# Another order of the beginning: quads 4 and 5 convolved ahead of W1's split, b2 split last, zero fills later

## The chip, the cores and the metric

One core of one Trainium2 chip runs the whole kernel. The metric is device time in microseconds, from the first to the last instruction and what little lies around them. Several executions are timed and their median is compared.

## What is computed

The kernel normalizes x (8192 rows of 128, in 128 graphs of 64 rows), runs one graph convolution with a residual, adds x again, normalizes once more, and runs a mixture of eight experts with two chosen for each row:

```python
n  = layernorm(x)
h  = layer_norm(n, ln_gamma, ln_beta)
x  = x + (n + relu(adj @ h @ W_rel + b_rel + h @ W_root))
m  = layernorm(x)
s  = m @ Wg.T + bg                  # 8 scores for a row
p, e = softmax over the 2 highest scores, and which experts they are
x  = x + sum over the two e of p * (relu(m @ W1[e].T + b1[e]) @ W2[e].T + b2[e])
```

x is 4.2 MB, adj 2.1 MB, W1 and W2 2.1 MB each, all fp32. The expert products are done with each operand split into a high and a low fp16 half.

## The kernel before

**Units.** A tile is 128 rows (two graphs), a quad is 4 tiles, and the 64 tiles lie in five groups of 8, 16, 16, 16 and 8 tiles (`GS`, line 24), so group 0 is quads 0 and 1, and group 1 is quads 2 to 5. A pass of the expert part (`p`) is 256 gathered rows of one expert.

**One quad's path.** DVE takes x's statistics (`stats_in`) and scales (`scales_in_first`, `scales_in_last`, 16 short dependent steps). DVE (`norm_in`) or ACT (`h0_make`) normalizes, ACT forms the first sum (`plus_norm`). PE transposes (`h0_transpose`), ACT copies out of PSUM (`hT_copy`), PE multiplies by W_rel (`relation`), ACT copies (`u_copy`), PE adds W_root and the adjacency product (`convolve`). DVE adds the result to X (`residual`), takes statistics (`stats_out`), makes scales for two quads at once in the beginning (`scales_out_first`, `scales_out_last`), and DVE or ACT normalizes again (`norm_out`). ACT writes the high halves (`split_high`), DVE the low halves (`split_low`), PE transposes (`xn_transpose`), ACT copies (`xnT_copy`), PE makes the scores (`score`), DVE copies them (`scores`). `pair_of_quads(n)` is residual to norm_out for quads n and n + 1.

**Routing of a group.** `route_first` and `route_second` find each row's two experts, PE counts them (`rank`), `route_slots` and `route_rows` turn that into row numbers (IDX, semaphore slots_made), `route_blocks` into the expert of each pass (experts_made) and the two weights. With IDX made, POOL writes the group's rows to HBM with 2 indirect DMAs for each tile (`scatter`, line 314). SP then loads them transposed (`load_rows`), PE runs the passes (`hidden`, `output`), ACT and DVE split the hidden layer (`high_half`, `low_half`), ACT copies and stores the result (`y_copy`, `store_y`), POOL fetches it for each row (`gather`, line 321), and DVE adds it (`combine`). The scattered rows of a group need their buffer in HBM filled with zeros first (`zero_rows`, 2.5 MB each, line 250).

**Weights.** W1 is split in 8 column blocks c of 512: PE multiplies by a masked identity (`weight_whole`), ACT writes the high half (`weight_high`), PE subtracts it (`weight_rest`), ACT writes the low half (`weight_low`); the 8 blocks go through PSUM banks `WB`, four at a time (`four_whole`, `four_rest`, `four_high`, `four_low`). W2 is split without PE: ACT `second_high`, DVE `second_low`, one per expert. b2 is split on one partition: two ACT copies and one DVE instruction at lines 841, 842 and 638.

**Order.** Every engine has its own written-out instruction list and waits on semaphores; nothing is planned by a program. The lists of the beginning are lines 255 to 283 for SP, 598 to 657 for DVE, 807 to 861 for ACT and 1022 to 1069 for PE. The loop over passes follows on each. Ahead of it PE waits for b1's rows, for both parts of b2 (`b2_made`, 2) and for the six quads' scores (`score_made`, 6); in pass 1, after `rank(1)`, it waits for all of W2's low halves (`w2lo_made`, 8). DVE has `route_slots(1)` and `route_rows(1)` at the end of its pass 0, after two low halves and 8 `stats_in` of group 2. The order of PSUM banks for quads 0 to 5 is given by `banks` (line 153): quad 2 has (PY, PH3), quad 3 (PH2, PC), quad 4 (PA, PB), quad 5 (PH0, PH1).

## Time and profile before

| | |
|---|---|
| median of 3 runs | 740.11 us (738.97 to 742.23) |
| the profiled execution | 739.89 us |
| its span, first to last instruction | 738.0 us |
| PE busy / weight loads | 397.4 / 332.7 us |
| DVE, ACT, POOL busy | 310.2, 241.7, 250.0 us |
| mean granted TensorE clock | 0.751 |
| first pass of the experts on PE | 86.33 us |
| indirect DMAs, POOL | 128 writing (44.43 us on), 128 reading |

A timeline row gives the start in us from the start of the span, the busy time of the merged instructions, engine, line, operation, output and inputs, shapes and count, and in brackets the idle time before it and what ended it. "issue" and "remote" (in the chain: "another core or an unknown queue") mean that nothing the profile shows ended the wait; on one core, "remote" is not another core. A wait's row in the list of waits gives total us, number of times, longest.

### The profile page before, as it was taken

The page shows a single profiled execution, that of the slowest core. Times are in us where ns is not written, and L with a number is a line of the kernel's source. Part 1 is how long each engine was busy: PE and PEld are TensorE (multiplying, and loading weights), DVE is VectorE, ACT ScalarE, POOL GpSimd, SP SyncE. Part 2 cuts the span into 40 slices and gives each one's busy share as a digit, 9 for nine tenths or more (in the row PEclk, how much of TensorE's full clock was granted, in tenths as well). Part 3 has the DMA queues.
Part 4 walks back from the last instruction along what each step waited for, and adds up shares of the span by engine and source line. Part 5 has one row for each costly group of instructions (what it writes and reads, how often), then busy time and mean ns, then how long its engine had stood idle before and what let it go on. Part 6 is the DMA issues. An engine that isn't in the chain of part 4 may idle for free.

```text
span 738.0 us, 12242 instructions
## 1 busy us (share of the span) xinstructions
PE 397.4 (54%) x3927; PEld 332.7 (45%) x3927; DVE 310.2 (42%) x1113; ACT 241.7 (33%) x519; POOL 250.0 (34%) x263
## 2 busy tenths in 40 slices
PE   4873652199728505987211139964801999415910
PEld 4652540198618404875100039853701887314700
DVE  6773870067707403568400005761400753203651
ACT  3875310178425202852100027621300553102300
POOL 2043047400340672002777700044375000672053
PEclk9996585599868855999655559995955899756965
DMA  9934022132221211133111123232331442421231
GB/s 306 368 142 116 0 54 82 33 73 66 55 64 38 78 50 50 36 79 73 50 53 53 50 61 73 64 75 61 73 82 43 112 117 62 104 53 47 67 106 53
DMA packets 86540, 59.48 MB, mean 81 GB/s; under 512 B 57426, under 2 KB 78546, under 8 KB 85844
## 3 DMA queue, kind: packets, MB, share of 16 engines
q1 hardware_dynamic: 56756, 31.23, 14.7%
q0 software_dynamic: 8192, 16.79, 8.0%
q10 hardware_dynamic: 21536, 10.69, 6.1%
q8 instruction: 38, 0.62, 0.3%
q14 instruction: 18, 0.15, 0.1%
HBM read 19.61 MB, written 28.38 MB: 65 GB/s over the span
## 4 chain that ended last, share of the span: by engine, by line
PE 40%; another core or an unknown queue 23%; issue 19%; DVE 9%; ACT 5%; POOL 2%; DMA 1%; ACTq 0%; SPq 0%; DVEq 0%; POOLq 0%
PE PH L990 6%; PE PY L1014 5%; PE PY L1019 5%; PE PY L1015 5%; PE PH L992 5%; PE PH L991 4%; PE PY L1006 2%; POOL YG L330 2%; PE PB L911 1%; ACT N L734 1%; DVE STI L384 1%; PE PA L919 1%; DVE HL L571 1%; PE PA L920 1%
## 5 line engine op out<-in xcount | busy, mean ns | idle before, releaser
L571 DVE SCALAR_TENSOR_TENSOR HL<-PH,HH 128x512 f16<-128x512 f32 (+1 forms) x168 | 108.4, 674 | 293.0 <-ACT HH L791 244.5
L317 POOL DMA_INDIRECT rows<-XHL,IDX x128 | 123.9, 968 | 264.5 <-DVE IDX L543 227.0
L330 POOL DMA_INDIRECT YG<-yrows,IDX x128 | 121.8, 951 | 211.8 <-DMA yrows<-YB 173.9
L791 ACT ACTIVATE HH<-PH 128x512 f16<-128x512 f32 (+1 forms) x168 | 95.6, 582 | 145.3 <-remote 95.8
L1015 PE MATMUL PY<-W2H,HL 128*128 x652 | 122.6, 231 | 18.5 <-issue 18.4
L1014 PE MATMUL PY<-W2H,HH 128*128 x652 | 122.6, 231 | 10.9 <-issue 10.7
L990 PE MATMUL PH<-XT,W1H 128*128 128x256 f16 (+1 forms) x396 | 107.1, 273 | 26.6 <-issue 24.8
L799 ACT ACTIVATE YB<-PY 128x256 f32<-128x256 f32 x84 | 31.8, 378 | 272.7 <-remote 167.2
L992 PE MATMUL PH<-XT,W1L 128*128 128x256 f16 (+1 forms) x396 | 106.1, 271 | 20.5 <-issue 20.5
L1019 PE MATMUL PY<-W2L,HH 128*128 x652 | 106.6, 231 | 18.0 <-issue 18.0
L991 PE MATMUL PH<-XT,W1H 128*128 128x256 f16 (+1 forms) x396 | 106.3, 271 | 17.4 <-issue 17.4
L1006 PE MATMUL PY<-B,KH 128*128 x99 | 27.0, 272 | 110.5 <-issue 62.7
L1015 PEld LDWEIGHTS PY<-W2H,HL 128*128 128x128 f16 x652 | 67.8, 104 | 15.8 <-issue 15.0
L1014 PEld LDWEIGHTS PY<-W2H,HH 128*128 128x128 f16 x652 | 67.4, 103 | 15.7 <-issue 13.2
L1019 PEld LDWEIGHTS PY<-W2L,HH 128*128 128x128 f16 x652 | 57.1, 104 | 23.2 <-issue 22.7
L1006 PEld LDWEIGHTS PY<-B,KH 128*128 128x128 f16 x99 | 10.0, 101 | 120.3 <-issue 118.8
L990 PEld LDWEIGHTS PH<-XT,W1H 128*128 x396 | 41.2, 104 | 46.8 <-issue 37.4
L992 PEld LDWEIGHTS PH<-XT,W1L 128*128 x396 | 40.8, 103 | 25.3 <-issue 20.5
L991 PEld LDWEIGHTS PH<-XT,W1H 128*128 x396 | 40.9, 103 | 23.1 <-issue 19.2
L590 DVE SCALAR_TENSOR_TENSOR X<-YG,PR,X 128x128 f32<-128x128 f32 x128 | 36.2, 347 | 17.2 <-DMA YG<-yrows,IDX 16.6
L460 DVE SCALAR_TENSOR_TENSOR XHL<-N,XHL 128x512 f16<-128x512 f32 x16 | 10.8, 690 | 47.3 <-issue 30.7
L727 ACT ACTIVATE X<-X,SHI,SC 128x128 f32<-128x128 f32 x64 | 26.1, 483 | 0.0
(186 smaller groups left out, 517.8 us busy)
## 6 DMA issues: line engine op xcount, KB each, us to landing
yrows<-YB ACTq DMA_DIRECT2D x37, 256.0 KB, 2.7
rows<-XT SPq DMA_DIRECT2D x2, 2496.0 KB, 15.5
YG<-in_w SPq DMA_DIRECT2D x2, 2048.0 KB, 11.8
out<-X SPq DMA_DIRECT2D x16, 256.0 KB
X<-in_x SPq DMA_DIRECT2D x3, 1024.0 KB, 5.5
ADJ<-in_adj SPq DMA_DIRECT2D x32, 64.0 KB, 3.2
rows<-XHL,IDX POOLq DMA_INDIRECT x128
YG<-yrows,IDX POOLq DMA_INDIRECT x128
```

What stands on the lines that cost most here:

```text
L317: nc.gpsimd.indirect_dma_start(rows[g % 2], bass.IndirectOffsetOnAxis(ap=IDX[:, col:col + 1], axis=0), XHL[:, src:src + 2 * P].bitcast(F32 ...
L330: nc.gpsimd.indirect_dma_start(YG[g % 2][:, dst:dst + P], None, yrows[g], bass.IndirectOffsetOnAxis(ap=IDX[:, col:col + 1], axis=0)).then_ ...
L571: nc.vector.scalar_tensor_tensor(layer(HL[:, at:at + 2 * BW], p), layer(PH[p % 2 * 2 + h][:, :], p), 0.0, layer(HH[:, at:at + 2 * BW], p), ...
L590: ins = nc.vector.scalar_tensor_tensor(tile(X, t), y, PR[:, pr:pr + 1], tile(X, t), ALU.mult, ALU.add)
L791: nc.scalar.activation(layer(HH[:, at:at + 2 * BW], p), layer(PH[p % 2 * 2 + h][:, :], p), ACT.Relu).then_inc((hia_made, hib_made)[h], 1)
L990: nc.tensor.matmul(o, wh, hi, start=True, stop=False)
L991: nc.tensor.matmul(o, wh, lo, start=False, stop=False)
L992: last = nc.tensor.matmul(o, wl, hi, start=False, stop=True)
L1006: nc.tensor.matmul(PY[:, k * n * P:(k + 1) * n * P], KH[:, H_B2M:H_B2M + P], b2, start=True, stop=False, skip_group_check=True)
L1014: nc.tensor.matmul(o, HH[:, at:at + P], wh, start=False, stop=False, skip_group_check=True)
L1015: nc.tensor.matmul(o, HL[:, at:at + P], wh, start=False, stop=False, skip_group_check=True)
L1019: last = nc.tensor.matmul(o, HH[:, at:at + P], wl, start=False, stop=c == C - 1, skip_group_check=True)
```

## The change

PE's list: after the scores of quads 0 and 1 come the transposes and relations of quads 4 and 5, `rank(0)`, and their convolutions; W1's split (both fours) follows, then quads 2 and 3's second transposes. W1's PSUM banks and waits change to fit. ACT's list: `h0_make(5)` ahead of `plus_norm(3)`; the copies of quads 4 and 5, `plus_norm(4)`, b1 and W1's first four; `plus_norm(5)` between its highs and lows; `norm_out(3)` and the split of quads 2 and 3 between the two fours; b2's copies after all quads, then `second_high` of experts 2 to 7 (0 and 1 earlier). DVE's list: `norm_in(4)` ahead of the scores of group 0; `residual` of quads 2 and 3 and their scales and `norm_out(2)` around `route_slots(0)` and `route_rows(0)`, ahead of `route_blocks(0)`; `residual` of quads 4 and 5 directly after b1; the low halves of W2 for experts 2 to 7 as one block at the end, behind group 1's first routing and b2. SP's list: the zero fill of buffer 0 after the adjacency loads of quads 4 and 5. `norm_in` has one wait more. Nothing is added to or taken from the computation.

```diff
--- before.py
+++ after.py
@@ -148,7 +148,7 @@
         PH = [pb(f"PH{k}") for k in range(4)]
         PY = pb("PY")
         PA, PB, PC = pb("PA"), pb("PB"), pb("PC")
-        WB = 2 * [PA, PB, PH[0], PH[1]]
+        WB = [PB, PH[1], PH[3], PC, PB, PH[1], PY, PH[2]]
 
         def banks(n):
 
@@ -267,10 +267,10 @@
             sp.dma_start(YG[1][:, :], w2[:, :]).then_inc(w2_in, 16)
             for r in (0, 32):
                 sp.dma_start(B2F[r:r + 1, :], b2[:, :]).then_inc(b2_in, 16)
-            zero_rows(0)
             for n in (4, 5):
                 sp.wait_ge(conv_done, n - 3)
                 load_adj(n)
+            zero_rows(0)
             zero_rows(1)
 
             sp.wait_ge(b1hi_made, 1)
@@ -410,6 +410,7 @@
                 if n >= 4:
                     dve.wait_ge(xnT_done, n - 3)
                     dve.wait_ge(xhi_made, n - 3)
+                    dve.wait_ge(xlo_made, n - 3)
                 for k in range(GT):
                     t = n * GT + k
                     at = 2 * T0[g] + GS[g] + t - T0[g]
@@ -623,38 +624,45 @@
             pair_of_quads(0)
             split_low(0)
             split_low(1)
+            norm_in(4)
             scores(0)
             scores(1)
             route_first(0)
             route_second(0)
-            norm_in(4)
+            residual(2)
+            stats_out(2, 0)
             route_slots(0)
             route_rows(0)
+            residual(3)
+            stats_out(3, 1)
+            scales_out_first(2, 2)
+            scales_out_last(2, 2)
+            norm_out(2)
             route_blocks(0)
 
             dve.wait_ge(b1hi_made, 1)
             nc.vector.scalar_tensor_tensor(B1L[:, :], B1F[:, :], W1S, B1H[:, :], ALU.mult, ALU.subtract).then_inc(b1lo_made, 1)
+            for i in range(2):
+                residual(4 + i)
+                stats_out(4 + i, i)
+            split_low(2)
+            split_low(3)
+            scales_out_first(4, 2)
+            scales_out_last(4, 2)
+            norm_out(4)
+            second_low(0, 2)
+            scores(2)
+            scores(3)
+            split_low(4)
+            split_low(5)
+            scores(4)
+            scores(5)
+            route_first(1)
+            route_second(1)
             dve.wait_ge(bt_made, 1)
             nc.vector.scalar_tensor_tensor(B2[32:33, :], B2F[32:33, :], YS / 64.0, BT[32:33, :],
                                            ALU.mult, ALU.subtract).then_inc(b2_made, 1)
-            pair_of_quads(2)
-            second_low(0, 1)
-            split_low(2)
-            split_low(3)
-            second_low(1, 2)
-            scores(2)
-            second_low(2, 3)
-            scores(3)
-            pair_of_quads(4)
-            second_low(3, 6)
-            split_low(4)
-            split_low(5)
-            second_low(6, 7)
-            scores(4)
-            second_low(7, 8)
-            scores(5)
-            route_first(1)
-            route_second(1)
+            second_low(2, 8)
 
             for p in range(NP):
                 for n, at in START.items():
@@ -828,36 +836,36 @@
                 split_high(n)
             for n in (0, 1):
                 xnT_copy(n)
+            h0_make(5)
             plus_norm(3)
-            h0_make(5)
-            four_high(0)
-            exp_gap(0)
-            four_low(0)
-            four_high(4)
-            four_low(4)
-            act.wait_ge(b1_in, 16)
-            nc.scalar.mul(B1H[:, :], B1F[:, :], W1S).then_inc(b1hi_made, 1)
-            act.wait_ge(b2_in, 32)
-            nc.scalar.activation(B2[0:1, :], B2F[0:1, :], ACT.Copy, scale=YS / 64.0).then_inc(b2_made, 1)
-            nc.scalar.activation(BT[32:33, :], B2F[32:33, :], ACT.Copy, scale=YS / 64.0).then_inc(bt_made, 1)
             for n in (4, 5):
                 hT_copy(n)
             for n in (4, 5):
                 u_copy(n)
-            second_high(0, 4)
+            exp_gap(0)
+            plus_norm(4)
+            act.wait_ge(b1_in, 16)
+            nc.scalar.mul(B1H[:, :], B1F[:, :], W1S).then_inc(b1hi_made, 1)
+            four_high(0)
+            plus_norm(5)
+            four_low(0)
             norm_out(3)
             for n in (2, 3):
                 split_high(n)
+            four_high(4)
+            four_low(4)
+            second_high(0, 2)
             for n in (2, 3):
                 xnT_copy(n)
-            for n in (4, 5):
-                plus_norm(n)
-            second_high(4, 8)
             norm_out(5)
             for n in (4, 5):
                 split_high(n)
             for n in (4, 5):
                 xnT_copy(n)
+            act.wait_ge(b2_in, 32)
+            nc.scalar.activation(B2[0:1, :], B2F[0:1, :], ACT.Copy, scale=YS / 64.0).then_inc(b2_made, 1)
+            nc.scalar.activation(BT[32:33, :], B2F[32:33, :], ACT.Copy, scale=YS / 64.0).then_inc(bt_made, 1)
+            second_high(2, 8)
             act.wait_ge(b2_made, 2)
 
             for p in range(NP):
@@ -943,8 +951,12 @@
 
             def weight_whole(c):
 
-                if c >= 4:
+                if c == 3:
+                    pe.wait_ge(rank_used, 1)
+                if c in (4, 5):
                     pe.wait_ge(wlo_made, c - 3)
+                if c >= 6:
+                    pe.wait_ge(conv_read, c - 3)
                 nc.tensor.matmul(WB[c][0:P - 1, :], KF[:, K_M:K_M + P - 1], YG[0][:, c * HID:(c + 1) * HID],
                                  start=True, stop=True).then_inc(w_done, 1)
 
@@ -1043,20 +1055,23 @@
                 xn_transpose(n)
             for n in (0, 1):
                 score(n)
+
+            pe.wait_ge(score_made, 2)
+            for n in (4, 5):
+                h0_transpose(n)
+            for n in (4, 5):
+                relation(n)
             pe.wait_ge(kh_in, 16)
+            rank(0)
+            for n in (4, 5):
+                convolve(n)
             pe.wait_ge(w1_in, 16)
-
-            pe.wait_ge(score_made, 2)
             four_whole(0)
-            rank(0)
             four_rest(0)
             four_whole(4)
             four_rest(4)
             pe.wait_ge(wlo_made, 8)
-            first_half(4, 5)
             for n in (2, 3):
-                if n == 3:
-                    pe.wait_ge(rank_used, 1)
                 xn_transpose(n)
             for n in (2, 3):
                 score(n)
```

## Rows read from the trace of the kernel before

**Rows 1.** The page, part 4: share of the span of the chain that ended last.

```profile
PE 40%; another core or an unknown queue 23%; issue 19%; DVE 9%; ACT 5%; POOL 2%; DMA 1%; ACTq 0%; SPq 0%; DVEq 0%; POOLq 0%
```

**Rows 2.** The list of waits from 98 us to the end, POOL's rows.

```profile
POOL rows L317 <- DVE IDX L543: 187.4, 4, 62.9
...
POOL YG L330 <- DMA yrows<-YB: 173.9, 4, 61.8
```

**Rows 3.** Busy times by stretch: W1's split, then two of POOL's runs of indirect DMAs.

```profile
core 0: us, PE busy (x) PEld busy (x) DVE busy (x) ACT busy (x) POOL busy (x), PEclk, DMA share, GB/s
33.40:45.70 12.30, 11.02 (x26) 4.62 (x26) 9.93 (x54) 9.47 (x21) 1.13 (x1) 0.87 0.14 57
44.40:66.20 21.80, 9.72 (x65) 7.79 (x65) 13.00 (x48) 11.17 (x21) 15.82 (x16) 0.87 0.47 170
98.90:144.00 45.10, 11.51 (x74) 7.03 (x74) 8.49 (x35) 1.62 (x4) 30.73 (x32) 0.58 0.21 60
```

**Rows 4.** Timeline of DVE, up to the first routing's end.

```profile
33.25 0.19 DVE L466 COPY LG<-PH 128x32 f32<-128x32 f32 x1 [0.70 <-PE PH L935]
...
38.81 0.22 DVE L504 COPY TOT<-PC 128x64 f32<-128x64 f32 x1 [1.17 <-PE PC L942]
...
43.96 0.17 DVE L543 CAST IDX<-SLF 128x16 int32<-128x16 f32 x1
...
46.54 0.19 DVE L636 SCALAR_TENSOR_TENSOR B1L<-B1F,B1H 128x32 f16<-128x32 f32 x1
```

**Rows 5.** Timeline of DVE, quads 2 to 5 and group 1's routing.

```profile
48.40 1.27 DVE L638 SCALAR_TENSOR_TENSOR B<-HL,HH 1x1024 f16<-1x1024 f32 x1 [1.66 <-issue]
...
52.83 0.17 DVE L373 TENSOR_TENSOR MEANO<-STO 128x8 f32<-128x8 f32 x1
...
56.52 1.11 DVE L453 TENSOR_SCALAR N<-X,SCO,SHO 128x127 f32<-128x127 f32 x4
...
60.77 1.29 DVE L460 SCALAR_TENSOR_TENSOR XHL<-N,XHL 128x512 f16<-128x512 f32 x2 [2.54 <-issue]
...
70.00 0.19 DVE L466 COPY LG<-PY 128x32 f32<-128x32 f32 x1 [7.34 <-PE PY L935]
...
79.43 1.88 DVE L580 SCALAR_TENSOR_TENSOR W2L<-YG,W2H 128x512 f16<-128x512 f32 x3
...
85.22 0.19 DVE L466 COPY LG<-PH 128x32 f32<-128x32 f32 x1 [0.92 <-PE PH L935]
...
92.31 0.28 DVE L504 COPY TOT<-PC 128x128 f32<-128x128 f32 x1
```

**Rows 6.** Timeline of ACT: b2's first copy, quad 2's second transpose, quads 4 and 5.

```profile
46.25 1.04 ACT L841 ACTIVATE B<-HL 1x1024 f16<-1x1024 f32 x1
...
67.45 0.59 ACT L758 COPY T<-PH 128x512 f32<-128x512 f32 x1 [6.19 <-remote]
...
78.40 1.64 ACT L734 ACTIVATE N<-X,SHO,SCO 128x127 f32<-128x127 f32 x4 [4.73 <-DVE SHO L446]
...
80.99 0.56 ACT L758 COPY T<-PB 128x512 f32<-128x512 f32 x1
```

**Rows 7.** Timeline of PE, start of the first pass.

```profile
86.33 0.39 PE L990 MATMUL PH<-XT,W1H 128*128 128x256 f16 x1 [1.14 <-DVE LG L466]
```

**Rows 8.** Timeline of POOL: first and 14th indirect DMA of group 0, first of group 1.

```profile
44.43 1.13 POOL L317 DMA_INDIRECT rows<-XHL,IDX  x1 [39.58 <-DVE IDX L543]
...
61.07 1.22 POOL L317 DMA_INDIRECT rows<-XHL,IDX  x1 [0.30 <-issue]
...
98.92 0.96 POOL L317 DMA_INDIRECT rows<-XHL,IDX  x1 [34.10 <-DVE IDX L543]
```

**Rows 9.** Timeline of SP's queue: first zero fill, first transposed loads.

```profile
13.95 0.62 SPq L252 DMA_DIRECT2D rows<-XT  x1
...
66.19 4.01 SPq L244 DMA_TRANSPOSE XT<-rows  x3
```

**Rows 10.** The page, part 2: traffic in slices of 18.45 us.

```profile
GB/s 306 368 142 116 0 54 82 33 73 66 55 64 38 78 50 50 36 79 73 50 53 53 50 61 73 64 75 61 73 82 43 112 117 62 104 53 47 67 106 53
```

## The prediction

> **What bounds the kernel now.** I read the chain that ended last first: 40% of it is PE's work, and 42% are "issue" and the unknown releaser, waits that nothing in the profile ends [rows 1]. Then the waits of POOL: its indirect writes wait for the row numbers IDX of each group, its reads for the stored results [rows 2]. Nothing behind the beginning waits for a fixed moment; each stage waits for the one before it. So what the beginning wins by the time POOL's second run of writes starts (98.92 us, [rows 8]) should come off the end one for one, unless stalls behind it change.
>
> The stalls have a pattern, in the busy times by stretch [rows 3]. While POOL works through a run of indirect DMAs, PE gets through about 70 matmuls (65 in 21.8 us, 74 in 45.1 us), then almost stops, and starts again when the run is over. In the first run one sees it begin: DVE pauses 2.54 us before a low half [rows 5], and ACT gets quad 2's transpose at 67.45 after 6.19 us [rows 6], 1.3 us after SP's first load, which itself waits for the scatter to land [rows 9]. In the old beginning PE has in this run both relations and both convolutions of quads 4 and 5 (48 matmuls), and 8 transposes before.
>
> Then I read DVE's timeline, since it carries the chain through the beginning: it waits 7.34 us for quad 2's scores up to 70.00 and ends the six quads' scores at 85.22; POOL's second run follows 13.70 us later [rows 5, 8].
>
> **The change, part by part.** I lay DVE's new list end to end, each piece with its old duration.
>
> To the first IDX: old, slots and rows run from 38.81 to 43.96 (5.15 us), behind 1.17 us of waiting for `rank(0)` and the 1.1 us of `norm_in(4)`, so routing's first half ended at 36.5 [rows 4, 5]. Now `norm_in(4)` falls into the waits for the first scores (0.70 us at 33.25 and a like one before it, [rows 4]). In its old place stand `residual(2)` and its statistics. Two quads' residuals and statistics run from the end of b2's instruction, 49.67, to 52.83 [rows 5], 1.58 each. So slots start at 36.5 + 1.58 = 38.1 and IDX is at 43.3, 0.7 earlier. On PE `rank(0)` now stands behind the transposes and relations of quads 4 and 5. From the scores at 33.4 ACT ends a sum (1.64) and a copy (0.6), and 16 matmuls follow at 9.72/65 = 0.15 [rows 3, 4, 6]: 38.0, just hidden. If it is 1 us late, so is all.
>
> From IDX on (43.4): `residual(3)` 1.58; scales of a pair 3.69 (52.83 to 56.52); `norm_out(2)` 1.1; `route_blocks(0)` with b1 2.7 (43.96 to 46.54 and 0.19) [rows 4, 5]; residuals of quads 4 and 5 3.16; two low halves 1.29; scales 3.69. That is 17.2 us, so the scales of quads 4 and 5 are there at 60.6; they were at 78.40 [rows 6]. From there to the last scores old needed 6.82 us (78.40 to 85.22) through ACT, PE and ACT [rows 5, 6]; DVE's own work beside it (norm 1.1, two W2 blocks at 0.63, two scores, two low halves 1.29) is 4.1 and fits. Last scores: 67.4, **17.8 us earlier**.
>
> Is ACT ready? Between 33.4 and 60.6 it has four normalizations or sums at 1.64, the 16 evictions of W1 at 9.47/16 = 0.59 or less, eight copies and splits and two W2 blocks at about 0.6: 22 us in 27 [rows 3, 6]. That leaves 5 us for its hand-overs with PE. b2's two ACT copies (1.04 each, [rows 6]) lie beside the last scores and the routing.
>
> What is paid back: group 1's row numbers used to follow the last scores by routing, low halves, statistics and slots, with no block of weights between (85.22, 92.31, 98.92). Now b2 (1.27) and six W2 low halves (six times 0.63 = 3.8) stand on DVE behind the routing and ahead of the first low half [rows 5]: **5.0 us given back**. PE itself starts when b2 is ready, at 67.4 + 4.2 + 1.3 = 72.9 against 86.33 [rows 7], 13.4 earlier, and its wait for W2 in pass 1 is over by then. The shift of POOL's second run is 17.8 - 5.0 = **12.8 us**.
>
> Zero fill: its issue moves from 13.95 [rows 9] to behind quads 4 and 5's adjacency, about 22 us. Old, all that was asked for in the first 24 us had moved by 37 us at 306 and 368 GB/s [rows 10]. Both fills (5.1 MB) from 22 us on take 14 us at the second rate and end at 36 to 38; POOL needs the first at 43.4. Hidden, with 5 us to spare; past that, each us late is a us of the end. The extra wait of `norm_in(4)` costs nothing, since the low half it names stands ahead of it on DVE.
>
> Not in this sum: stalls inside POOL's first run. Old they cost DVE 2.54 us and the chain 6.19. New, PE has fewer matmuls in it: by the code, of W1 the last block's two, four rests, eight wholes and four rests, then 24 for quads 2 and 3, 24 for quads 4 and 5: about 66, against the 65 that it got through before. So the limit is met only at the very end, if at all. Below the sum nothing is to be gained but PE at its higher clock there (the granted share is 0.87 in the first run's stretch, 0.58 in the second, [rows 3]). Above it: one pause like DVE's, 2.5 us. I take 0.8 us, nearer to none. Net: 12.0 us.
>
> A rule that speaks against it. POOL's DMAs of the first run come every (61.07 - 44.43)/13 = 1.28 us while DVE is busy 13.0 of 21.8 us, and one that meets DVE's low half takes 1.22 instead of about 0.96 [rows 3, 5, 8]. The Trainium skill (SBUF — State Buffer, "Who interferes with whom") says that a DVE instruction with two SBUF inputs and a GpSimd one that reads SBUF lock each other out for a whole instruction. DVE will be denser in this run, with four such low halves and two of W2; at the 0.26 us of the row each, the run would end 1.6 us later by the rule, and 0 by the even pace of the others. The run's end is off the chain of the sum, so neither changes it.
>
> **The rivals.**
> B, *PE's hand-overs of quads 4 and 5 are held to the end of the run.* Old, ACT got its transpose only 1.34 us behind the landing of the scatter [rows 6, 9]. With a run 0.7 us earlier that is 66.7, and from the first such copy to the last scores it is 80.99 to 85.22, 4.23 us [rows 5, 6]: last scores 70.9, 3.5 later than in the sum. Gain 12.8 - 3.5 = 9.3, span 728.7. For it: 66 matmuls are right at the limit, and completions lagged before PE stopped. Against: they are spread over 20 us here.
> C, *the gain is eaten behind the beginning.* The eight later sets of POOL's DMAs (four writing, four reading, each with its wait in [rows 2]) may meet PE at other points. If they turn out 6 to 9 us worse in sum, the span is 732 to 735. Against: from POOL's second run on the instruction lists are the same and their distances too.
> D, the slower side: *W1's split chokes inside the run.* Old, the split lay ahead of it (33.4 to 45.7, [rows 3]) and convolutions, which need one signal for four tiles, lay in it. Now twelve of sixteen evictions wait for PE's signal one by one, under the run. If these signals are held to its end from the first lows on (47 us in my layout), then 20.4 us of the way to the last scores start at 66.7: 87.1, 1.9 later than old, and with the 5.0 given back the span is 738 + 6.9 = 745. It decides from a first hold before about 50 us. Against: the W1 signals fall among the first 18 of the 65 matmuls that PE gets through before it is held [rows 3].
> E, *more*: PE stays at the higher clock to the last scores, and these come 2 to 3 us sooner (quads 4 and 5's eight transposes and sixteen score matmuls); 723.
> F, it doesn't do what it says: `rank(0)` behind the new work comes late enough to push IDX and everything back by the same; 1 to 2 us, inside the others' ranges.
>
> **How the numbers follow.** The likeliest is the sum: 738.0 - 12.0 = 726.0 us of span; the profiled execution has 1.9 us around its span, and the median stands 0.2 above the profiled 739.9. Forecast 728.1. Chances: sum (A) 0.45, B 0.27 (731), C 0.12 (734 to 737), D 0.08 (742 to 747), E 0.08 (725). From 722 to 736 holds A, B, E and half of C. About 0.5% (3.7 us) is what a measurement of this kernel can tell from no change: faster than 736.4 are A, B, E and most of C, 0.86; within, the rest of C and the mild part of D and stalls I don't see, 0.08; slower 0.06.
>
> **What would show it.** IDX's first copy at 43.3 and the first indirect DMA at about 43.7. Scales of quads 4 and 5 at 60.6 (ACT's L734, third time). Last L466 of the six at 67.4 (A) or about 71 (B). The first pass's matmul at 72.9, POOL's second run at 86.1. ACT's W1 rows without "remote" ahead of them; with 5 us or more of it there, D. The distance from POOL's second run to the end of the span is 639.1 us before; if it is within 2 us of that, C is out. If the second run starts at 86 and the span is still above 733, my step "one for one" is wrong; if it starts after 92, the layout of DVE's list or the stalls in the first run are.

## The result, and the profile after

The median went from 740.87 to 734.72 us (five runs each side, ratio 0.9917, interval 0.9898 to 0.9937). Another pair on another chip gave 744.96 and 739.77 us, ratio 0.9911 (0.9874 to 0.9948). So the change gains 5 to 6 us of time where 12 were forecast; the forecast median was 728.1. The profiled execution has a span of 733.4 us against 738.0.

| | before | after | forecast |
|---|---|---|---|
| first IDX copy | 43.96 | 45.30 | 43.3 |
| scales of quads 4 and 5 (SHO) | 78.20 | 68.87 | 60.6 |
| last scores of the six quads | 85.22 | 75.90 | 67.4 |
| first matmul of the first pass | 86.33 | 82.41 | 72.9 |
| POOL's second run starts | 98.92 | 94.66 | 86.1 |
| from there to the end of the span | 639.1 | 638.8 | 639.1 |

The timeline of DVE in the changed kernel, at the scales of quads 4 and 5 (start, duration, engine and line, operation; in brackets the idle time before it and what ended that):

```profile
58.02 0.68 DVE L461 SCALAR_TENSOR_TENSOR XHL<-N,XHL 128x512 f16<-128x512 f32 x1
58.62 0.21 DVE L373 TENSOR_TENSOR MEANO<-STO 128x8 f32<-128x8 f32 x1
...
59.23 0.17 DVE L377 SCALAR_TENSOR_TENSOR VARO<-MDIFO,VARO 128x8 f32<-128x8 f32 x1
59.97 0.17 DVE L437 TENSOR_SCALAR RAO<-VARO 128x8 f32<-128x8 f32 x1 [0.57 <-issue]
60.68 0.17 DVE L363 TENSOR_SCALAR RTO<-RAO 128x8 int32<-128x8 int32 x1 [0.54 <-DVE RAO L437]
61.40 0.17 DVE L364 TENSOR_SCALAR SCO<-RTO 128x8 int32<-128x8 int32 x1 [0.54 <-DVE RTO L363]
62.79 0.17 DVE L367 TENSOR_TENSOR RTO<-SCO 128x8 f32<-128x8 f32 x1 [1.22 <-DVE SCO L364]
...
68.60 0.17 DVE L369 SCALAR_TENSOR_TENSOR SCO<-RTO,SCO 128x8 f32<-128x8 f32 x1
68.87 0.17 DVE L447 SCALAR_TENSOR_TENSOR SHO<-MEANO,SCO 128x8 f32<-128x8 f32 x1
```

Up to 59.23 the steps start 0.2 us apart or closer; from 59.97 they are 0.70 or 1.40 apart, though each lasts 0.17 us, and at 68.60 they are 0.2 apart again. The chain of scales took 10.25 us (58.62 to 68.87) instead of 3.69. POOL's first run, in its timeline, frames this:

```profile
45.77 1.13 POOL L317 DMA_INDIRECT rows<-XHL,IDX  x1 [40.91 <-DVE IDX L544]
...
58.63 0.96 POOL L317 DMA_INDIRECT rows<-XHL,IDX  x1 [0.30 <-issue]
...
64.95 0.96 POOL L317 DMA_INDIRECT rows<-XHL,IDX  x1 [0.30 <-issue]
```

The steps slow down beside its twelfth DMA and recover 2.7 us after its last has been issued. Below, a "hold" is this: an engine starts its instructions late though nothing that the profile shows stands in their way. The windows of the changed kernel show the same by engine (stretch, its length, then busy time and number of instructions of PE, PE's loads, DVE, ACT and POOL, the granted clock of PE, DMA share, GB/s): up to 59 us the engines are dense, then DVE and ACT thin out, while PE has matmuls for 5.16 of the 7 us, at about half its clock. ACT's copy of quad 3's second transpose starts at 63.51, after 3.13 us of "issue"; PE's 8 matmuls that read it follow at 64.15. The last line is a stretch in POOL's second run, 21 matmuls in 32 us.

```profile
45.70:59.00 13.30, 9.20 (x24) 3.41 (x23) 12.20 (x54) 12.44 (x27) 10.19 (x11) 1.00 0.32 97
59.00:66.00 7.00, 5.16 (x24) 4.62 (x24) 1.52 (x9) 1.97 (x4) 5.39 (x6) 0.53 0.82 333
...
101.95:133.90 31.95, 5.44 (x21) 1.60 (x18) 1.72 (x5) 1.19 (x2) 24.04 (x26) 0.58 0.25 70
```

Behind the beginning, in the timelines of DVE, PE and POOL, which answer to [rows 7] and [rows 8]:

```profile
75.90 0.19 DVE L467 COPY LG<-PH 128x32 f32<-128x32 f32 x1 [1.52 <-PE PH L943]
...
80.44 1.22 DVE L663 SCALAR_TENSOR_TENSOR B<-HL,HH 1x1024 f16<-1x1024 f32 x1
...
82.41 0.39 PE L1002 MATMUL PH<-XT,W1H 128*128 128x256 f16 x1 [6.55 <-DVE B L663]
...
94.66 0.96 POOL L317 DMA_INDIRECT rows<-XHL,IDX  x1 [28.75 <-DVE IDX L544]
```

The last scores come 9.3 us earlier. From them to POOL's second run it is 18.76 us against 13.70: the 5.06 us of b2 and W2 that were given back.

### The profile page after: what moved, and what is told of

Its sections match the earlier page's. It is cut to its first block, busy times and chain, and to the rows that moved or that the text cites. A ratio compares the mean times of both kernels' runs of the same rounds, so it can differ in the third digit from the quotient of the medians.

```text
span 733.4 us, 12242 instructions
## 1 busy us (share of the span) xinstructions
PE 400.7 (55%) x3927; PEld 338.3 (46%) x3927; DVE 310.4 (42%) x1113; ACT 241.0 (33%) x519; POOL 249.8 (34%) x263
## 4 chain that ended last, share of the span: by engine, by line
PE 36%; another core or an unknown queue 20%; issue 20%; DVE 15%; ACT 5%; POOL 2%; DMA 2%; ACTq 0%; SPq 0%; DVEq 0%; POOLq 0%
PE PY L1026 5%; PE PH L1002 5%; PE PY L1031 5%; PE PY L1027 5%; PE PH L1004 4%; PE PH L1003 4%; PE PY L1018 2%; POOL YG L330 2%; PE PB L919 2%; DVE HL L572 2%; ACT N L742 1%; DVE STI L384 1%; ACT N L724 1%; DVE STO L431 1%
## 5 line engine op out<-in xcount | busy, mean ns | idle before, releaser
L1027 PE MATMUL PY<-W2H,HL 128*128 x652 | 124.1, 233 | 22.1 <-issue 21.9
L1026 PE MATMUL PY<-W2H,HH 128*128 x652 | 124.2, 233 | 16.0 <-issue 15.9
L1031 PE MATMUL PY<-W2L,HH 128*128 x652 | 108.1, 233 | 18.7 <-issue 18.7
L919 PE MATMUL PB<-WF,T 128*128 128x128 f32 x96 | 16.7, 330 | 21.1 <-ACT T L750 21.1
```

The lines of the kernel that those rows point to most:

```text
L1026: nc.tensor.matmul(o, HH[:, at:at + P], wh, start=False, stop=False, skip_group_check=True)
L1027: nc.tensor.matmul(o, HL[:, at:at + P], wh, start=False, stop=False, skip_group_check=True)
L1031: last = nc.tensor.matmul(o, HH[:, at:at + P], wl, start=False, stop=c == C - 1, skip_group_check=True)
```

## The experiments

Times of key instructions come from each kernel's profiled execution. "This chip's before" is the kernel before, run beside. Two theories stand at the start: R, POOL's run slows DVE's steps and that ate the gain (as S in the expectations, with one allowance of instructions for all engines together); X, the loads of later x, issued in this stretch, do it (DMA share 0.82 in the windows above). P stands for any cause on PE's side. Theory O, that the order was never worth what I wrote, came up on the way.

**e1_scatter_held**, the changed kernel, POOL's first run held until the six quads are scored:

```diff
                 pool.wait_ge(zero_out[g % 2], 16)
+                if g == 0:
+                    pool.wait_ge(score_made, 6)
```

> The changed kernel, but POOL's first run of indirect DMAs also waits for the scores of all six quads. Nothing is left out. In the changed kernel the 16 dependent steps of quads 4 and 5's scales stretch over 10.25 us (58.62 to 68.87), most of them 0.70 or 1.40 us apart, where the same steps of quads 2 and 3 took 3.7 us. Theory S (POOL's run slows every engine once a common allowance of instructions is used up): without the run beside it the chain takes 3.7 us again, no start on PE is delayed by 'issue', the last scores come at about 69.3 instead of 75.9, and the run itself ends at about 90, so the first pass starts 10 to 14 us later than 82.4 and the span is about 743 to 748. Rival X (the chain is slow for another reason in that place, as the 2.5 MB of x that SP loads from 55 us on): it still takes about 10 us and the last scores stay at 75.9.

749.08 us beside 746.43. The scales took their usual time (SHO at 59.72), and DVE's timeline has the last scores where my layout put them (67.4):

```profile
66.75 0.19 DVE L469 COPY LG<-PH 128x32 f32<-128x32 f32 x1 [1.51 <-PE PH L945]
```

The list of pieces was laid out rightly; the run costs the new order 9.15 us at this point (up to 1.8 of it a later start, since IDX was at 43.47 here), and 10.75 beside e13 below, the changed kernel on e1's own chip. Holding it costs more, as the run then stands in the chain: second run at 106.0.

**e2_sp_waits**, 120 satisfied waits on SP's queue, to see whether SP's instructions matter:

```diff
+            sp.wait_ge(w_rest, 4)
+            for _ in range(120):
+                sp.wait_ge(kf_in, 16)
```

> The changed kernel with 61 more instructions on SP, which has nothing else to do there: waits on a semaphore that has long been reached, from the fourth low part of W1 (about 49.4 us) on, ahead of SP's wait for b1. No engine waits for them. Theory S (the allowance in POOL's run is common to all engines, about 190 instructions from the run's start at 45.8, used up at about 60 us): 61 more instructions use it up some 5 us earlier, at about 55; residuals and low halves of quads 4 and 5 and the second four of W1 slow down too, the last scores come 2 to 6 us after 75.9, and the span grows by as much. Rival P (each engine, or PE alone, has its own allowance, as I had assumed in the prediction): nothing changes by more than 0.5 us on DVE, ACT and PE; the slow steps still begin at 59.97. Rival T (the slowing begins at a time after the run's start, about 14 us, whatever has run): the same as P.

740.27 us. Slow steps from 58.67, 13.2 us into the run. But the trace has 60 instructions for the 120 waits, and SP ran them off from 42.7 to 46.8 us, mostly before the run began, so this tells little.

**e3_rank_between**, `rank(0)` between the relations of quads 4 and 5, and **e4_w2_spread**, W2's blocks on ACT and DVE ahead of the last scores instead of behind the routing (DVE's part is shown; on ACT `second_high(2, 8)` goes ahead of `norm_out(5)`):

```diff
+            relation(4)
             pe.wait_ge(kh_in, 16)
             rank(0)
+            relation(5)
```
```diff
+            second_low(2, 4)
             scores(4)
+            second_low(4, 6)
             scores(5)
...
-            second_low(2, 8)
+            second_low(6, 8)
```

> The changed kernel with rank(0) between the relations of quads 4 and 5 instead of behind both. In the changed kernel DVE waits 1.11 us for it (40.13) and the row numbers come at 45.30. Theory: the wait goes (relation of quad 4 ends at 38.3, DVE is free at 39.0), IDX comes 1.1 us earlier, POOL's first run starts at 44.7, and what hangs on it follows by about 1 us; the span is 0 to 1.5 us shorter, which is near to what three rounds can tell. If the first run ends the slow steps, the last scores come 1.1 us earlier even though the steps before them do not: the end of the run decides. Rival: the last scores are set by the number of instructions alone, and the gain is under 0.3 us.

> The changed kernel with W2's high parts of experts 2 to 7 on ACT ahead of norm_out(5), where ACT waits 4.97 us, and four of the six low halves on DVE ahead of the last two score copies, where DVE waits 1.41 and 1.52 us; two low halves stay behind the routing. Step tested: 'b2 and six low halves give back 5.0 us' (18.76 us from the last scores to POOL's second run against 13.70 before). If that step is right, 2.5 us of it go: the distance is 16.3 us and the span 2 to 3 us shorter (about 731). Rival: these instructions now stand in the slow stretch and cost 0.7 us each there, so that the last scores come later by what is won, and the span does not change.

e3: 738.64 us, ratio 0.9914 (0.9879 to 0.995), no better than the change itself. IDX came at 43.35 and the run at 43.8, but the slow steps came earlier too, from 57.07, and the last scores at 75.49. The early start was worth under half a microsecond. e4: 737.95, ratio 0.9914 (0.9886 to 0.9942). The last scores to the second run took 18.7 us (77.16 to 95.84) where I expected 16.3: a miss. PE's first pass waits for b2 (6.54 us, to 83.67), and DVE, earlier done with W2, waits 1.61 and 0.53 us for ACT's first high halves instead. W2's blocks on DVE had lain beside other work of almost their length.

**e5_x_later**, the later loads of x issued behind the first four transposed loads (72.1 us), outside the run:

```diff
-            for g in range(2, G):
-                load_x(g)
...
+                if ch == 3:
+                    for g in range(2, G):
+                        load_x(g)
```

> The changed kernel with SP's loads of x for groups 2 to 4 (2.5 MB) behind the first four transposed loads instead of at 55.07 us, inside POOL's first run. In four runs with the change's order the slow steps began 3.9 to 4.2 us after these loads were issued, and also 13.2 to 13.5 us after POOL's run began; those two are tied to each other there. Rival X (the loads of x beside POOL's writes start the slow stretch): it does not come, the steps of quads 4 and 5's scales take 3.7 us, the last scores come at about 69.5, POOL's second run at 88, and the span is 6 us shorter (about 727). Theories S and T (POOL's run alone does it): the slow steps still begin about 13.5 us into the run, nothing moves by more than 1 us, span 732 to 735.

739.92 us, ratio 0.9953 (0.9924 to 0.9982). The windows of the same stretch:

```profile
59.00:66.00 7.00, 2.62 (x13) 2.29 (x11) 1.15 (x6) 0.69 (x2) 4.82 (x6) 0.50 0.17 53
```

DMA share 0.17 instead of 0.82, and yet DVE has 6 instructions, slow from 58.43, and the last scores come at 76.66. X is refuted.

**e6_pe_dummies**, 30 small matmuls into an unused place ahead of W1's second four blocks:

```diff
             four_rest(0)
+            pe.wait_ge(conv_read, 3)
+            for _ in range(30):
+                nc.tensor.matmul(PY[:, 0:E], KH[:, H_ID:H_ID + P], KH[:, H_ID:H_ID + E], start=True, stop=True)
             four_whole(4)
```

> The changed kernel with 30 extra tiny matmuls (128 rows, 8 columns, fp16) on PE in POOL's first run, ahead of the second four of W1, into a bank that is free there. PE waits 1.58 us there; the extra work takes 1 to 2 us, so PE's own list moves by less than 1 us. Theory S (one allowance of about 150 to 190 instructions for all engines in a run): 60 instructions more (30 weight loads, 30 matmuls) use it up at about 54 to 56 us instead of 59.3; residuals, low halves and W1's lows slow down, last scores 77 to 80. Theory P (PE has its own allowance of about 140): PE reaches it at about 62 instead of never, and DVE's slow steps do not begin earlier. Theory T (a time into the run): slow steps still from 13.2 to 13.5 us into the run, last scores at 76 to 76.5.

747.39 us (one run) beside 743.35. Now ACT is held, and PE, whose subtraction reads what ACT writes, starts behind it. From their timelines:

```profile
50.79 0.59 PE L960 MATMUL PH<-YG,KF 128*127 128x512 f32 x1
62.37 0.60 ACT L774 ACTIVATE W1H<-PB 127x512 f16<-127x512 f32 x1 [10.72 <-issue]
63.02 0.69 PE L966 MATMUL PB<-W1H,KH 127*127 127x512 f16 x1 [11.64 <-issue]
```

That is rival D's choke, brought about: W1's split stops inside the run, and the kernel is 4.0 us slower than the one before (D: 7). Its last scores, at 80.48, come earlier than D had them (87.1), since the first four blocks were split, and the second four's `weight_whole` done, before the hold. Whether ACT or PE's signal to it was late, the profile doesn't tell. In the change itself this doesn't occur. DVE's steps slow at the same place as without the dummies, 13.2 us into the run, so DVE isn't slowed by what PE has issued, and S, one allowance for all engines, is refuted.

**e7_run_paused**, the run interrupted after ten DMAs until the scales of quads 4 and 5 are made; **e8_paused_spread** adds e3 and a form of e4:

```diff
                 for t in range(GS[g]):
+                    if g == 0 and t == 5:
+                        pool.wait_ge(scale_made, 6)
```

> The changed kernel with POOL's first run in two parts: 10 indirect DMAs as before, then a wait for the scales of quads 4 and 5, then the other 6. In all theories but X the slow stretch needs the run to be longer than the 10 DMAs (12.6 us): the scales come at about 62.5 instead of 68.87, the other 6 DMAs run from 62.7 to 70.3, the last scores come at 69.3 to 71, the rows of the first chunk are there at about 74, the first pass starts at 76 (82.41 before), POOL's second run at 88 to 89 (94.66), span 727 to 728. If a second part slows PE at once (an allowance that does not come back in a pause of 4 us), the last scores come at 73 and the span is 730. Theory X (loads of x): no gain from it, span 733 or more.

> The paused run with rank(0) between the two relations and four of W2's six last low halves in DVE's waits before the last score copies (their high parts around ACT's norm_out(5)). If the terms add: 1.1 us from rank(0), 2.5 us from W2, on top of the pause, so POOL's second run starts at about 85 and the span is 723 to 725. Rival: the first chunk's rows or PE's transposes become the bound, and no more than 1 us comes on top of the pause.

e7: 730.57 us, ratio 0.9841 (0.978 to 0.9902); by the ratios better than both kernels, though its interval just touches that of the change (from 0.9898). Scales at 61.36, last scores at 68.39, first pass 74.97. POOL's second run, in its timeline:

```profile
87.18 0.96 POOL L319 DMA_INDIRECT rows<-XHL,IDX  x1 [17.28 <-DVE IDX L546]
```

and the end 639.1 us later. e8: 730.97 (0.979 to 0.992), a span of 729.1 where I expected 723 to 725; the second half of its run was stretched (one DMA took 2.30 us beside dense DVE and ACT work), so the rows came late for the first pass (76.99), and the second run started at 89.2.

**e9_early_pause, e10_before_held, e11_rank_first, e12_slots_first** ran on another chip, and there the kernel before takes 481.27 us. e9 is the change with the pause after the fourth DMA, until W1's eighth part is split:

```diff
+                    if g == 0 and t == 2:
+                        pool.wait_ge(wlo_made, 8)
```

> The changed kernel; GpSimd's first run of sixteen indirect DMAs is cut after the fourth (before, in run e7, after the tenth) and goes on when ScalarE has split W1's eighth tile (wlo_made 8), near 59 us. It asks what the onset of the slow steps on VectorE, 13.2 us after the run's start in every run so far, follows. Theory N (number of DMAs issued since the start, about eleven): after four DMAs and a pause from 50 to 59 us the steps of the scales of quads 4 and 5 (58.6 to 62.3) lie beside DMAs 5 to 7 and are not slowed (SHO of quads 4 and 5 at 61 to 62.5, last scores at 68 to 69.5), and slow steps begin only about seven DMAs into the second part, near 67. Theory T (time since the first DMA): they are slow from 59.3 as in the changed kernel, SHO at 68 to 70. Theory B (the DMAs lie too densely for too long, and a pause lets it drain): no slow steps before 59 + 13 = 72. The second part ends near 59 + 12 x 1.27 = 74.3 us (more if its DMAs are held themselves), so the first pass has its rows near 79 and the second run stands near 91 to 93; the end 639 us later, 730 to 732.

> The kernel before with GpSimd's first run held until the scores of six quads are made, as e1 did it to the changed kernel (last scores there at 66.75 us). The difference of the two at the last scores is what the new order is worth without a run beside it. If the order is worth what I wrote (17.8 us) and the run cost the kernel before nothing at that point: last scores at 84 to 85.5. If the kernel before lost there too (ScalarE's 6.19 us wait on a remote semaphore at 67.45 and what followed): 76 to 80, the order alone then being worth 10 to 13 us, and the run taking 6 to 9 from either kernel. The end is late in both cases, since the run itself (20 us) now stands behind the scores: last scores + 39 us to the second run, as in e1, and 640 us from there: 755 to 765.

> Run e7 (the run cut after the tenth DMA until the scales of quads 4 and 5 are made; 730.57 us, second run at 87.2), and in addition TensorE takes the ranks of the second group's tokens ahead of the first pass instead of behind its second pass's first half, and VectorE the slots behind the first pass's two subtractions and ahead of the statistics of two quads (1.5 us). In e7 the mask was ready at 72.9 and the ranks were read at 80.58. Expected: slots start at 79.0 instead of 80.6, second run at 85.6 to 86, end 1.2 to 1.6 us earlier than e7's: 728.5 to 730, if the distance from the second run to the end (639 us) holds when the second run comes forward without the scores. If not the second run but the first pass (74.97) set the end: no gain, 730 to 731.

> As e11, and VectorE computes the slots of the second group ahead of the last six parts of W2's split. The slots then end near 81 (mask 72.9, b2 until 74.2, ranks from 75, 6.1 us of slots), the second run starts at 81 to 82, 5 to 6 us ahead of e7's; the W2 parts end at 84 to 85 instead of 77.8, so the first pass's output (79.4 in e7) waits for them until about 85, with the second pass's behind it. If the distance from the second run to the end holds (the cause of the end as I predicted it): end near 721, time 724 to 726. If the passes set it (first output 5.6 us late and PE behind it): no better than e7, 730 to 733. Between: the run now lies beside the dense second and third passes, whose instructions it can hold.

e10 is e1's edit in the kernel before. With the run out of the way its last scores, by DVE's timeline, are at

```profile
75.78 0.19 DVE L468 COPY LG<-PH 128x32 f32<-128x32 f32 x1 [0.92 <-PE PH L937]
```

against 66.75 in e1: **the order alone is worth 9.03 us**, not 17.8. And the run costs the kernel before 85.22 - 75.78 = 9.44 us, the new order 9.15. e9 took 479.56 us and e10 503.76. No comparison of spans is drawn from e10, since its chip differs from e1's; up to the last scores neither kernel has a run beside it.

e11 and e12 start from e7:

```diff
             pe.wait_ge(score_made, Q0[2])
+            rank(1)
             before = None
...
+            route_slots(1)
+            route_rows(1)
             second_low(2, 8)
```

They take `rank(1)` ahead of the first pass; e12 computes group 1's slots ahead of W2's last blocks (the second part of the diff), e11 behind the first pass's subtractions. 474.64 (ratio 0.9868, 0.9831 to 0.9906) and 472.23 (0.9814, 0.9779 to 0.985). The windows of e12 in POOL's second run:

```profile
85.10:119.80 34.70, 33.05 (x392) 30.91 (x393) 26.75 (x104) 24.42 (x55) 26.16 (x29) 0.94 0.31 88
```

392 matmuls beside 29 indirect DMAs. In POOL's first run, the four profiles from this chip show no engine held at all. So e9 (last scores at 68.97, nothing slow) couldn't answer its question there.

**e13_after_same_chip and e14_before_profiled** are the two kernels unchanged, **e15_slots_first_again and e16_early_pause_again** e12 and e9 once more; all on a chip that does hold.

> The changed kernel as it is, beside the kernel before on the same chip. If this chip holds no engine in GpSimd's runs (kernel before near 481 us): theory O (the order alone is worth 9.0 us at the last scores, whatever the run does, and 5.06 are given back by b2 and W2 behind the routing) expects last scores at 66.7 to 68, the second run 4 us ahead of the kernel before's, and a gain of 3 to 5 us (476 to 478.5). Theory R (the run beside the new order ate the forecast gain of 17.8 us at the last scores, of 12 at the end) expects the forecast itself here, 11 to 13 us (468 to 470). If the chip does hold them (740 us): as the first comparison, ratio 0.990 to 0.994, and last scores at 75 to 77 us.

> The kernel before, unchanged, profiled on this chip. Where no engine is held: theory O expects its last scores at 75.5 to 77.5 us (in e10, with the run held back, 75.78), 9 us behind the changed kernel's, and its second run at 89 to 91. Theory R expects them at 84 to 85.5 as in the first profile, with the second run at 98 to 99. Where engines are held: 83 to 86 and 97 to 100 by both.

> e12 once more (the run cut after ten DMAs, ranks and slots of the second group ahead of the first pass and of W2's last six parts). On a chip that holds no engine: ratio 0.981 as before (472.23 beside 481.27). On a chip that does: the second run at 80 to 83; its twenty microseconds then lie beside the dense passes 1 to 3, whose hold begins 5 to 9 us into a run. If the end follows the second run one for one (639 us, or 664.5 from the second part as e7's list counts it: 639.1 from 87.2): end near 721, time 722 to 726, ratio 0.972 to 0.978. If the hold falls on W2's last parts and the first pass's outputs: nothing over e7, ratio 0.983 to 0.986.

> e9 once more (the run cut after its fourth DMA until W1's eighth part is split, near 59 us), which says nothing where no engine is held in any case (then: scales at 61 to 62, last scores at 68 to 69.5). On a chip that holds them: theory N (number of DMAs, about eleven) scales of quads 4 and 5 not slowed, SHO at 61 to 62.5, slow steps from about 67; theory T (13.2 us from the first DMA) slow from 59, SHO at 68 to 70; theory B (dense for too long, drained by the pause) none before 72.

e13: 739.77 us, last scores at 77.50; e14: 742.12, last scores at 87.17, and its second run at 100.85, both just above what was expected. The last scores are 9.67 us apart, near what e1 and e10 show without a run (9.03). But O and R had expected the same of this pair on a chip that holds, so it doesn't choose between them. What speaks for O is e10 beside e1; the pair of unchanged kernels on a chip without holding wasn't tried.

e15: 728.02 us beside 744.96, ratio 0.9784 (0.9733 to 0.9834). Its second run starts at 80.80, 6.4 us earlier than e7's, but the end is no earlier in the two profiles (726.2 and 726.3): from the second run it is 645.4 us, no longer 639. (Where the list behind the second run is the change's own, this distance was 638.8 to 642.9, but 646.3 in e6; the change and e13, one program, lie 4.0 apart.) By this distance alone the 6 us may therefore be scatter, and by the medians e15 is, if anything, ahead of e7 (0.9784 against 0.9841, the intervals overlap). What can be seen is what the earlier run lies beside; here is e15's window next to that of e12, the same program:

```profile
85.50:120.70 35.20, 11.81 (x71) 8.13 (x72) 8.83 (x41) 1.68 (x4) 26.67 (x29) 0.60 0.17 53
```

71 matmuls instead of 392 beside the same 29 DMAs. A run that starts 6.4 us earlier beside dense passes also holds them earlier, which could cost what its start wins. That "one for one" holds only for an order that shifts as a whole is an argument from this, and not shown.

e16 against e9 is one program on two chips. Timelines of ACT, first e9's, then e16's:

```profile
64.70 0.59 ACT L768 COPY T<-PB 128x512 f32<-128x512 f32 x1
65.56 0.59 ACT L768 COPY T<-PH 128x512 f32<-128x512 f32 x1 [0.27 <-PE PH L936]
```
```profile
66.71 0.59 ACT L768 COPY T<-PB 128x512 f32<-128x512 f32 x1 [2.14 <-PE PH L936]
68.84 0.59 ACT L768 COPY T<-PH 128x512 f32<-128x512 f32 x1 [1.54 <-remote]
```

737.22 us (one run) beside 744.96. Both go alike until 64.9 (the low halves ahead of the last scores start at 64.31 and 64.32). The scales are not slowed (SHO at 61.69), which refutes this expectation's theory T, and the hold comes between the ninth and the tenth DMA, 6 us after the break, which refutes its theory B with 13 us; N (eleven DMAs, near 67) is nearest but early. Last scores at 76.00: the pause in this place gains nothing, the hold only meets the next link of the chain.

**e17_breaks_of_four and e18_breaks_of_two**: e15, and in all later runs POOL fills a scratch row after every fourth DMA (three fills, 2.8 us) or every second (one fill, 1.4 us):

```diff
+            def pause(i):
+                if i % 2 == 0:
+                    nc.gpsimd.memset(PZ[:, :], 0.0).then_inc(paused, 1)
+                    PAUSED[0] += 1
+                    pool.wait_ge(paused, PAUSED[0])
```

> e15 with a break of about 2.8 us (three fills of a scratch row on GpSimd) after every fourth indirect DMA of all runs but the first, which has its own pause. A run of 32 then lasts 39 + 7 x 2.8 = 59 us and one of 16 28 us; the runs' total grows from 317 to some 460 us. Theory U (what counts is the unbroken stretch; in the dense passes engines are held only from 4.7 us on, which is the fourth DMA): no engine is held any more, and the time falls towards the chip without holding, bounded by GpSimd's chain: 520 to 620 us. Theory D (what counts is the mean density or a total, breaks of this size don't refill anything): engines stay held as before and the run is longer, 760 to 880 us. On a chip that holds no engine: 500 to 560, slower than its 472.

> The same with a break of 1.4 us (one fill) after every second DMA: the same mean density, stretches half as long. Theory U: as e17 or a little better, 520 to 620. Theory D: as e17, 760 to 880. If a break must have a certain length to help (e7's was 6 us, e16's 9.3 us): e18 is clearly slower than e17, by over 30 us.

599.26 us beside 740.09 (ratio 0.8106, 0.8002 to 0.821) and **592.18 us (0.801, 0.7967 to 0.8053)**, two timed runs each. e15 is in both: it had given 0.9784, the breaks the rest. POOL does 158 us of idle fills in e18 and the kernel is a fifth faster. The page of e18: the chain that ended last by engine, POOL's fills, and a matmul of the second layer (count | busy us, mean ns | idle before it and what ended it):

```profile
POOL 52%; DVE 15%; PE 13%; issue 12%; ACT 3%; DMA 2%; SPq 0%; ACTq 0%; POOLq 0%; DVEq 0%
...
L311 POOL MEMSET PZ<- 1x1600 f32 x111 | 157.8, 1421 | 0.1
...
L1042 PE MATMUL PY<-W2H,HH 128*128 x652 | 122.0, 231 | 0.6 <-issue 0.6
```

and of the changed kernel, the chain and the same matmul:

```profile
PE 36%; another core or an unknown queue 20%; issue 20%; DVE 15%; ACT 5%; POOL 2%; DMA 2%; ACTq 0%; SPq 0%; DVEq 0%; POOLq 0%
...
L1026 PE MATMUL PY<-W2H,HH 128*128 x652 | 124.2, 233 | 16.0 <-issue 15.9
```

PE's "issue" wait ahead of those matmuls is gone, and so are the chain's 20% of unknown releasers. POOL is the bound now. In the windows, 56 us of e18's second run (62 us long with its breaks):

```profile
86.70:142.90 56.20, 35.81 (x426) 33.44 (x426) 33.73 (x122) 28.89 (x66) 47.69 (x43) 0.83 0.21 59
```

426 matmuls pass beside it. Both times lie where theory U (the unbroken stretch) had them, 520 to 620, and far from D's 760 to 880; breaks of 1.4 us are enough, and e18 isn't slower than e17, it is 7 us faster. One rival stays: both kernels also lower the mean rate of the DMAs, from one per 1.27 us to about one per 2 us, and no run spreads them evenly. So it isn't shown that the stretch counts and not the rate.

## Why the prediction was wrong

**To the first IDX: 43.3, measured 45.30.** Not wrong as a sum. The same or nearly the same instructions gave 43.1 to 43.8 in e1, e3, e6, e7 and e15 and 44.6 to 45.7 in e11, e13, e14 and e16, the unchanged kernel before among the latter. The "just hidden" `rank(0)` isn't hidden when PE does the relations at its lower clock: from 35 to 40 us the granted clock is 0.51 to 0.55 in the change, e11, e13 and e16, where DVE waits 1.0 to 1.1 us for it, and 0.76 to 0.84 in e1, e7 and e15, where it waits 0.2 or less. This is what rival F said, of 1 to 2 us; e3 shows that under the hold it matters for the end by less than half a microsecond.

**DVE's list from IDX on: right.** From `residual(3)`, right behind IDX at 45.38, to the first step of the last scales is 13.24 us, as summed (60.6 - 3.69 - 43.4 = 13.5). With no run beside it, e1 ends the scores at 66.75 (forecast 67.4). From the scales to the last scores: 7.03 (6.82).

**The step that failed is the 0.8 us put for "stalls inside POOL's first run".** It measured 9.15 us (e1 against the change; 7.3 if the later IDX is taken out), 6.6 of it in the stretched scales. I argued from PE's count, 66 matmuls against a limit of 65 to 70, and PE, with 48 matmuls in the run by the windows, indeed wasn't what stopped the chain: its one late start there, 64.15, follows ACT's late copy and ends before the scales do. But the rows already had DVE pausing 2.54 us and ACT getting its transpose 6.19 us late [rows 5, 6]; I read these as consequences of PE's stop, and they were the same hold on other engines. A list without PE's work doesn't escape it. The old order lost 9.44 us to it, which I had counted among what the new order saves: 17.8 = 9.0 of order + 9.4 of hold - 0.6 (67.4 against 66.75). The hold stayed, in another place. With it in the sum, measured from the forecast scores (75.90 - 67.4 = 8.5, where 0.8 had been put): 12.8 - 8.5 = 4.3 us at POOL's second run, which is what came (98.92 - 94.66 = 4.26).

**Given back: 5.0, measured 5.06.** Right, though not for the reason written. e4 took four of the six low halves away from there and gained nothing. What sets the stretch is the order behind it: e12 and e15, with `rank(1)` and the slots ahead of the first pass and of W2's blocks, have 12.9 us from the last scores to the second run instead of 18.76.

**One for one: right here,** 638.8 against 639.1 us; C, which wanted 6 to 9 us more, is out. That it meets to 0.3 us is luck: the same program has 642.8 in e13, where the second run is 4.61 us ahead of e14's and the end only 1.2.

**Zero fills: hidden,** as said; POOL waited for IDX, not for them.

**The rule of the Trainium skill** (SBUF — State Buffer, "Who interferes with whom"): in the change the sixteen DMAs came every 1.28 us with DVE busy 12.2 of 13.3 us, and only the first two took over 0.97 us. The 1.6 us that I took from the rule didn't appear here. The same section infers that a GpSimd DMA's descriptors need the write side of the shared ports, which a VectorE instruction with two SBUF inputs leaves free; I had left that out, and the even pace agrees with it. In e8 a DMA beside DVE's low halves did take 2.30 us; why is open.

**The rivals.** B had the right suspect, a hold to the end of the run, but on PE's hand-overs and at 3.5 us instead of 8.5: 70.9 for the last scores, 75.90 measured. One hand-over was late, quad 3's to ACT (3.13 us of wait here, 7.97 in e13), but beside the scales and not in the chain. D needed 30 more matmuls to happen (e6). C and E didn't happen. The range, 722 to 736, has the 734.7 in it because it was drawn over B and half of C; A's own sum alone would have missed by 6.6 us.

**What stays open** is what exactly the hold follows. In ten kernels with the new order and an unbroken or late-paused first run (the change, e2 to e8, e13, e15) DVE is slowed first at nearly the same place of its list, its 58th to 60th instruction in the run, 13 to 14 us in; ACT in e6 8.1 us in; PE in dense passes after 5 to 9 us, ACT in e16 6 us after a pause of 8.4 us. Neither time, nor the number of DMAs, nor one engine's count explains them all. Nor is it known why one chip shows none of it. More instruction traffic isn't seen: on the pages of the change and of e12 (no hold) the queues "instruction" have the same 38 and 18 packets. (The Trainium skill, "Runtime: NRT & Kernel Launch", section "Instruction fetch mechanics", says that each engine refills its instructions by a DMA queue of its own, in blocks, and that this is mostly hidden.) A refill that comes late behind POOL's DMAs would fit a hold of any instruction, but the DMA records speak against it: in the change no packet of these queues starts between 47.5 and 89.9 us, so none arrives in or at the end of the hold from 59.4 to 68.4 us, and in e9, which has no hold, the same two packets lie at 47.1 and 86.4.

## What to carry to other kernels

A stall seen beside a foreign engine's run is a price of that run, not of the work it happened to hit: before a new order is credited with its disappearance, both orders should be set out without the run (two kernels with one wait each do it), and the cost of the run put back into both. And if several engines wait for "issue" or an unknown releaser while GpSimd issues indirect DMAs back to back, try to break the run up first: with a fill of 1.4 us after every second DMA, on top of e15, this kernel took 592.18 us instead of 740.09, while e15 itself (the new order, one pause in the first run, earlier slots) had taken 2% off. On a chip that shows no hold the breaks weren't tried.

## What the runs showed of the hardware

- Where the kernel before takes 740 us and more: while GpSimd issues indirect DMAs every 1.27 us without a break, VectorE's steps of 0.17 us start 0.70 or 1.40 us apart from 13 to 14 us on (timeline above), and TensorE's matmuls likewise in the second run (in the change at 102.28, 102.99, 104.40 and 105.82 us). ScalarE is held too (3.13 us in the change, 7.97 in e13), with too few instructions to see a step.
- The same program takes 472.23 us on one chip and 728.02 on another (e12, e15), and the kernel before 481.27 against 740 to 746; up to the hold, at 64.9 us, e9 and e16 start each instruction within 0.2 us of each other.
- A pause moves the hold: ten DMAs, 5.0 us of pause and six more leave the scales almost untouched (one gap of 1.05 us), four DMAs, 8.4 us and twelve do so for the scales but not for the transposes at 64.9.
- PE's granted clock averages 0.60 in the held stretch of e15, where PE is busy a third of the time and mostly at the lower of its two levels (1.2 and 2.4 GHz), and 0.94 in the same stretch of e12, where it is busy throughout. One kind of matmul (line 1027, 128 by 128) takes 314 ns there on average and 231 in e12. So a hold is paid a second time in matmuls at the lower clock.
